# Delta-rule kernel on one core: the state of two heads as one 128x128 block-diagonal operand

## What is computed

```
x = x + attn(layernorm(x));  x = x + ffn(layernorm(x))
# attn, for each head, from S = 0:
q, k, v = conv and silu of x @ Wq, Wk, Wv; q, k rotated and normalised
for each token:
    o    = q S + D (q.k) v
    S'   = alpha (S - beta k (k S)) + beta k v
y = (x @ Wg) * silu(rmsnorm(o) * w);  return y @ Wo
# ffn: softmax attention with 16 heads of 8 columns,
#      then the best 2 of 8 experts (128 -> 512 -> 128, gelu)
```

## Time and profile before

| what | value |
|---|---|
| runs of the kernel, lowest, median, highest | 7932.8, 7937.8, 7957.8 us |
| span of the profiled execution, first to last instruction | 7946.7 us |
| its mean granted TensorE clock | 0.70 of 2.4 GHz |
| busy: TensorE products, weight loads | 77%, 55% |
| busy: VectorE, ScalarE, GpSimd | 60%, 38%, 34% |
| instructions | 128119 |
| DMA | 30.2 MB, mean 4 GB/s |

### The profile page before, as it was taken

One profiled execution on the slowest core, in us unless ns is written; L12 is line 12 of the kernel. 1 busy time (PEld: TensorE's weight loads), 2 busy tenths in 40 slices (PEclk: granted clock), 3 DMA queues, 4 the chain that ended last, 5 costly groups with the idle time before them and its releaser, 6 DMA issues.

```text
span 7946.7 us, 128119 instructions
## 1 busy us (share of the span) xinstructions
PE 6133.5 (77%) x41472; PEld 4339.3 (55%) x41472; DVE 4732.0 (60%) x11688; ACT 3013.4 (38%) x5573; POOL 2662.6 (34%) x2989
## 2 busy tenths in 40 slices
PE   5787877877877778778787777787777877878777
PEld 3555554555545655546555456554565545655555
DVE  5655566655566555665556765556655566555662
ACT  2333334433344433343333443334333334333343
POOL 3333223433233332333322343323433233332331
PEclk6677666776667776667776677666777667766667
DMA  1000000000000000000000000000000000000000
GB/s 61 2 2 3 3 2 2 3 3 3 2 2 3 3 3 3 2 2 2 3 3 2 2 3 3 3 2 2 3 3 3 3 2 2 2 3 3 2 2 3
DMA packets 26490, 30.22 MB, mean 4 GB/s; under 512 B 4072, under 2 KB 22768, under 8 KB 25328
## 3 DMA queue, kind: packets, MB, share of 16 engines
q1 hardware_dynamic: 25712, 20.49, 0.8%
HBM read 16.29 MB, written 4.19 MB: 3 GB/s over the span
## 4 chain that ended last, share of the span: by engine, by line
PE 43%; issue 29%; POOL 15%; DVE 9%; ACT 3%; POOLq 1%; SPq 0%; DVEq 0%; ACTq 0%; DMA 0%
PE bank L852 42%; POOL NP L589 4%; POOL Gam L617 4%; POOL Gam L614 3%; POOL NP L586 2%; DVE NP L1245 2%; DVE NP L1378 2%; DVE hn L1231 1%; POOL NP L592 1%; PE bank L856 1%; POOL frstd L655 1%; ACT Gam L743 1%; ACT NP L689 1%; DVE Gam L1397 1%; DVE lpp L1265 0%
## 5 line engine op out<-in xcount | busy, mean ns | idle before, releaser
L852 PE MATMUL bank<-QK 64*128 64x256 f32 (+1 forms) x4096 | 1378.4, 466 | 260.0 <-ACT pT L815 108.5
L852 PEld LDWEIGHTS bank<-QK 64*128 64x128 f32 (+1 forms) x4096 | 611.4, 183 | 863.3 <-ACT pT L815 262.8
L1245 DVE SCALAR_TENSOR_TENSOR NP<-bank,conv_w,NP 128x255 f32<-128x255 f32 (+2 forms) x2304 | 929.6, 471 | 78.1 <-ACT NP L689 78.1
L839 ACT ACTIVATE QK<-bank,b 128x256 f32<-128x256 f32 x1024 | 422.7, 470 | 1176.5 <-PE bank L852 1175.0
L852 PE MATMUL bank<-mT,W 128*128 128x256 f32 x2048 | 671.0, 489 | 0.1
L852 PE MATMUL bank<-xnT,Wqkv 128*128 128x256 f32 x1536 | 583.3, 527 | 108.5 <-DVE NP L1245 53.5
L1563 DVE SCALAR_TENSOR_TENSOR moe<-bank,wsel,moe 128x128 f32<-128x128 f32 x512 | 156.1, 347 | 847.4 <-PE bank L852 847.4
L852 PE MATMUL bank<-NP,head_cols 128*32 128x256 f32 x1536 | 206.8, 484 | 498.3 <-POOL NP L586 498.2
L852 PE MATMUL bank<-W,QK 128*128 128x128 f32 x4096 | 538.0, 287 | 22.5 <-DVE moe L1563 22.5
L743 ACT COPY Gam<-NP 32x256 f32<-32x256 f32 x512 | 321.1, 627 | 612.3 <-DVE fac L1385 607.8
L852 PEld LDWEIGHTS bank<-W,QK 128*128 128x128 f32 x4096 | 525.9, 203 | 47.8 <-DVE moe L1563 28.6
(11 more groups left out here) (211 smaller groups left out, 11626.7 us busy)
## 6 DMA issues: line engine op xcount, KB each, us to landing
xin<-in_x SPq DMA_DIRECT2D x33, 128.0 KB, 2.1
out<-moe SPq DMA_DIRECT2D x32, 128.0 KB, 1.8
W<-in_W SPq DMA_DIRECT2D x1, 2048.0 KB
NP<-in_c_q_sel SPq DMA_DIRECT2D x1, 1536.0 KB, 8.7
NP<-in_c_k_sel SPq DMA_DIRECT2D x1, 1536.0 KB, 11.9
NP<-in_c_alpha_sel SPq DMA_DIRECT2D x1, 1024.0 KB, 5.4
Wqkv<-in_Wq SPq DMA_DIRECT2D x1, 512.0 KB, 12.7
Wqkv<-in_Wk SPq DMA_DIRECT2D x1, 512.0 KB, 13.2
```

The costliest lines, as they stand in the source:

```text
L839: ins = s.activation(h1[:, n % 2, f, :], ps[:, q, :], ACT.Gelu_apprx_tanh, bias=b1[:, n, f:f + 1])
L852: return mm(out_, lhsT, rhs, start=first, stop=last)
L1245: v.scalar_tensor_tensor(acc[:, n % 2, m, j:T], ps[:, m, 0:T - j], conv_w[:, kind, c, PAD - j:KT - j], acc[:, n % 2, m, j:T], ALU.mult, AL ...
```

## The change

S becomes [128, 8, 128]: for each pair of heads a 128x128 block-diagonal matrix, the even head's state in rows 0 to 63 and columns 0 to 63, the odd head's in rows and columns 64 to 127, and zeros elsewhere. GpSimd writes the zeros once, at the start. ScalarE copies the state in two instructions, one for each parity, 64 partitions each. A half of KS or QS is now 4 products of 128x128 by 128x128 for heads 0 to 7 or 8 to 15, and all that reads the banks goes by `HALF` in place of `PARITY`.

```
-        S = sb("S", [P, NC, DH])
+        S = sb("S", [P, NC, 2 * DH])
...
-        PARITY = [slice(0, H, 2), slice(1, H, 2)]
...
+            g.memset(S[:], 0.0).then_inc(pool_consts, 1)
+            pool.wait_ge(pool_consts, 9)
...
-                    g.tensor_tensor(R[:, PARITY[half], :], V[:, 1, PARITY[half], :], R[:, PARITY[half], :],
+                    g.tensor_tensor(R[:, HALF[half], :], V[:, 1, HALF[half], :], R[:, HALF[half], :],
...
-                    g.tensor_tensor(Dv[:, PARITY[half], :], Dv[:, PARITY[half], :], Kt[:, PARITY[half], :],
+                    g.tensor_tensor(Dv[:, HALF[half], :], Dv[:, HALF[half], :], Kt[:, HALF[half], :],
...
             act.wait_ge(loaded, 16 * len(loads))
+            act.wait_ge(pool_consts, 9)
...
-                        s.copy(S[:], by_head(ps)).then_inc(a_S.sem, 1)
+                        for q in range(2):
+                            ins = s.copy(S[rows_of(q), :, q * DH:(q + 1) * DH], by_head(ps)[rows_of(q)])
+                        ins.then_inc(a_S.sem, 1)
...
-                for k in range(8):
-                    h = 2 * k + half
-                    ins = product(by_head(ps)[:, k, :], QK[rows_of(h), h // 2, kind, TOK[1]],
-                                  S[rows_of(h), h // 2, :])
+                for k in range(4):
+                    c = 4 * half + k
+                    ins = product(ps[:, k * P:(k + 1) * P], QK[:, c, kind, TOK[1]], S[:, c, :])
...
-                v.tensor_tensor(Kt[:, PARITY[half], :], by_head(bank(("QS", half))), bc(Gc[:, 1, PARITY[half]], DH),
+                v.tensor_tensor(Kt[:, HALF[half], :], by_head(bank(("QS", half))), bc(Gc[:, 1, HALF[half]], DH),
...
-                            v.tensor_tensor(R[:, PARITY[half], :], by_head(ps), bc(Gc[:, 0, PARITY[half]], DH), ALU.mult)\
+                            v.tensor_tensor(R[:, HALF[half], :], by_head(ps), bc(Gc[:, 0, HALF[half]], DH), ALU.mult)\
```

More of the change, by code:

```diff
@@ L558, in _ @@
             g.memset(GT[:], 1.0).then_inc(pool_consts, 1)
-            pool.wait_ge(pool_consts, 8)
+            g.memset(S[:], 0.0).then_inc(pool_consts, 1)
+            pool.wait_ge(pool_consts, 9)
             pool.wait_ge(loaded, 16 * len(loads))
@@ L858, in _ @@
             pe.wait_ge(loaded, 16 * len(loads))
-            pe.wait_ge(pool_consts, 8)
+            pe.wait_ge(pool_consts, 9)
             pe.wait_ge(act_consts, 6)
@@ L1213, in _ @@
             dve.wait_ge(vec_consts, 1)
-            dve.wait_ge(pool_consts, 8)
+            dve.wait_ge(pool_consts, 9)
             dve.wait_ge(act_consts, 6)
```

## The result

The changed kernel takes 7588.4 us (median of 4 runs, 7569.6 to 7605.8) where the kernel before takes 7937.9: ratio 0.9549, 95% interval 0.9527 to 0.9571. The direction and the mechanisms of the state stage were right, the size was not.

What follows compares the result with a forecast made beforehand. TensorE was taken to bound the state stage. Per batch, 42.7 + 195.0 + 0.6 = 238.3 against 244.9 us gave -205 over 31 batches; with -5.5 for batch 0, 7937.8 - 210 = 7728 us, range 7620 to 7860.

Steps and rivals of the forecast that it cites:

- The records: State stage on TensorE: fewer, full-size products by S shorten KS by 1.33 us and each QS by 0.95, -3.2 us a batch.
- the oddity of KS's 0.55 us: KS's 32 records take 3.31 us, not twice 1.93; records overlap for 0.55 us, possibly where its halves meet.
- The second copy: ScalarE before KS: copying S in two parts adds 0.58 us a batch, wholly exposed, with no extra price for the stride.
- No new wait: Engines after KS and QS: no new wait but the copy's; the nearest, for W, worth at most 0.95 us.
- The clock in the state stage: Half-clock drops behind poorly filled products by S mostly vanish; the state stage goes from 49.9 us on average to 42.7.
- my allowance for a short drop: State stage: 0.8 us kept for one short half-clock drop in every other batch where products stay poorly filled.
- The rest of the batch: Stretches between state stages: carried over unchanged at 195.0 us each, plus 0.6 for the copy; they now last 191.1 to 198.6.
- batch 0: First batch, at half clock: half as many records save some 6.1 us, the copy costs 0.6, together -5.5 us.
- The clock falls as before: Rival for the state stage: only records are saved and clock drops remain, -86 us, 7850 us; chance 0.22.
- The rest also gains: Rival: stretches between state stages settle near 191.5 us, a further -105 us, 7620 us; chance 0.10.
- Slower: Rival: every batch meets the low clock, stages of 50.4 us and stretches between of 198.6, +146 us, 8084 us; chance 0.04.
- Nothing gained: Rival for KS and QS: two old records cost one padded record, leaving only the copy, +19 us, 7957 us; chance 0.04.

Runs made afterwards that it cites:

- The interleaved run: Kernel before with unpadded S and one copy, KS and QS each issuing both halves together, alternating row groups and banks; ratio 0.9537 to the kernel before.
- the paired heads: Changed kernel with the key products of an even and an odd head issued alternately in the per-head stretch; ratio 0.9622 to the kernel before.

## Why the prediction was wrong in size

**The records: right.** -3.2 us a batch forecast, 7.17 - 3.87 = 3.30 measured. The interleaved run also confirms what the oddity of KS's 0.55 us had said.

**The second copy: right.** 0.58 us, fully exposed, no price for the stride.

**No new wait: right.** TensorE runs from 2272.40 to the last expert without another wait than the 0.70 us that was there.

**The clock in the state stage: right in kind, too small.** The drops vanished, and the tests above show what had stood ahead of them. I had 42.7 us; it is 41.26. Of the 1.4 us, 0.8 was my allowance for a short drop where the last solve and the output products stay poorly filled: none came. The other 0.6 is the price of half-clock time: 48.22 - 41.26 - 3.30 = 3.66 us for the 6.8 us of the usual stage, 0.54 each, where I had taken 0.45 from the difference between long and usual stages. Together 45 us.

**The rest of the batch: the step that failed.** "The number would be most wrong through the 195 us that I carry over unchanged", I wrote, and so it was: 195.6 with the longer wait forecast, 192.4 measured, 100 us of the 159 by which the span's change exceeds the forecast. I had seen that these stretches lasted 191.1 to 198.6 us with the same instructions, and still took the old mean as the new one and half the spread as the likeliest case's range. What the runs show in its place is the per-head stretch: 32.6 us for 35.4, at a higher granted clock. The remainder is batch 0: it saved 18.2 us and not 5.5. Its state stage, 39.0 us and all at half clock before, is now 20.6 us with 5.0 at half clock.

**The rivals.** "The clock falls as before" is refuted by 31 stages at 1.00. "The rest also gains" was the nearest, at 7620 us with a chance of 0.10; the outcome combines it with a better stage. (Its further gain, recorded as -105 us, is 31 x -3.5 = -108.5 and does not move the 7620.) "Slower" would have needed long stages, and none came. "Nothing gained" took a 64-row product at half the cost; that is true when row groups and banks alternate, but not of the old order.

**What stays open.** That the per-head stretch takes 30 to 39 us by the granted clock is shown in every profile. That small delays move totals out of proportion is shown: waits longer by 0.25, 0.74 and 1.5 us a batch gave the old kernel -0.7, +1.3 and +2.6%, and one shorter by 0.43 us, with a copy moved to VectorE, cost the new one 1%. Which place the batches of a given kernel settle at I can't derive. So the 349 us are in their larger part the change's own (state stages: 268 of the span's 369), and the 82 us of the rest are partly chance of place: profiles of the changed kernel put the rest between 191.6 and 193.0, of the old one at 195.0 and 195.4. Chance alone it is hardly: over the 16 profiles whose stages or waits are given here (all but that of the paired heads), the per-head stretch has a mean of 34.9 to 37.7 us where KS or QS goes by 64 rows in the old order, and of 31.5 to 34.7 where neither does. Why the one goes with the other no run shows.

## What to carry to other kernels

In this kernel products of 64 rows waste the array twice. A record takes as long as a full one (0.12 us), and the granted clock falls behind a run of them though TensorE is fully busy. Pair them into full ones or alternate the row groups and banks, whichever costs less around it. Where a program's clock changes between stages, price a change by stages and by clock, give the untouched stages the full spread that they show now, and don't trust a gain or loss of 1% until a harmless delay of 0.4 us has been tried on both kernels. A freed wait is worth nothing by itself: the split copy saved 0.43 us a batch and the run was 80 us slower.

## What the runs showed of the hardware that I had not expected

- The clock fell behind 3.93 us of 64-row products with TensorE busy all the time (50 records, QS by 64 rows), and did not fall behind 3.84 us with 49 records where QS used 128 rows. The Trainium skill ("TensorE: Matmul & The Clock Gate", Why this matters for your kernels) ties the fall to idle gaps; here it came without a gap too, and also behind an idle wait of 2.77 us among full products.
- 64x64 f32 products in alternating row groups and banks run at 0.06 us a record (32 in 1.93 us), against 0.12 one row group at a time.
- The same program on four chips had medians from 7932 to 8011 us, and on one chip single executions from 7889 to 8019.
- VectorE and ScalarE read different halves of the partitions of one PSUM bank at the same time, in 695 and 580 ns. ScalarE's copy takes 580 ns alone too; VectorE's alone stands in no run.
